# Routing ranks: from one pass on VectorE before the routed attention to comparisons on GpSimd and sums on TensorE inside it

## The reference, cut to what matters

```python
def route(x, routing_token, num_tokens, k_eff):
    s = jnp.einsum('bnd,rd->brn', x, routing_token)[:, 0]
    scores = coor_descent(s, k_eff)
    sel_scores, sel_idx = jax.lax.top_k(scores, num_tokens)
    sel_scores = sel_scores + jax.lax.stop_gradient(1.0 - sel_scores)
    return (sel_scores, sel_idx)
...
sq, iq = route(x, rt_q, NQ, min(NQ * FETCH_K, SEQ))          # NQ = 128
...
routed_out = routed_out * sq[..., None]
out = jnp.broadcast_to(null_q, x.shape)
out = out.at[batch_idx, iq].set(routed_out)
return light + out
```

## Time and profile before

| | us |
|---|---|
| median of 3 runs (range) | 1854.55 (1852.1 to 1854.71) |
| profiled execution, its own time | 1848.03 |
| its span, first to last instruction | 1845.9 |
| main attention, until its last work | 364.84 |
| from there to the first work of the routed attention | 23.9 |
| routed attention | 388.7 to 749.4 |

### The profile page before, as it was taken

The page is one execution under the profiler, slowest core; times in us unless marked ns, Lnnn a source line. Parts: engine busy times, 40 slices in busy tenths (PEclk is TensorE's granted clock), DMA queues, the critical chain, the costliest instruction groups (busy, mean ns, idle before and its releaser), DMA issues. The chain is left out here.

```text
span 1845.9 us, 32031 instructions
## 1 busy us (share of the span) xinstructions
PE 1560.9 (85%) x10886; PEld 1093.7 (59%) x10886; DVE 1187.4 (64%) x3102; ACT 1005.5 (54%) x2685; POOL 371.4 (20%) x381
## 2 busy tenths in 40 slices
PE   3799999849999999499999986489979946899974
PEld 2477777626666666367777764355546722555543
DVE  5599997547777777544454534666642366889954
ACT  2488887606656666244444443124444435888935
POOL 0100000000000000021111034254403410788820
PEclk9899999959999999699999998689999968899978
DMA  4000000040000000110000012200001120333300
GB/s 136 1 1 1 1 1 1 1 135 1 1 1 1 1 1 1 65 56 10 8 9 10 20 55 87 109 16 13 15 23 46 46 82 7 87 87 86 91 13 23
DMA packets 43837, 62.50 MB, mean 34 GB/s; under 512 B 7432, under 2 KB 29776, under 8 KB 42864
## 3 DMA queue, kind: packets, MB, share of 16 engines
q1 hardware_dynamic: 39136, 51.08, 9.3%
q0 software_dynamic: 4544, 9.38, 1.4%
HBM read 49.88 MB, written 15.75 MB: 36 GB/s over the span
## 5 line engine op out<-in xcount | busy, mean ns | idle before, releaser
L561 ACT ACTIVATE probs<-psum_all,pair_negmax 128x256 f32<-128x256 f32 x512 | 235.4, 472 | 161.6 <-DVE pair_negmax L660 89.6
L1992 POOL TENSOR_TENSOR weighted<-state,c_all 128x512 f32<-128x512 f32 x128 | 163.5, 1297 | 87.4 <-DVE state L2002 72.8
L660 DVE TENSOR_REDUCE pair_negmax<-psum_all 128x2 f32<-128x512 f32 x192 | 123.7, 686 | 67.6 <-PE psum_all L476 67.6
L2002 DVE TENSOR_TENSOR_SCAN state<-decay,psum_all 128x512 f32<-128x512 f32 x128 | 149.0, 1200 | 14.9 <-PE psum_all L1920 12.0
L686 DVE TENSOR_SCALAR probs<-probs,pair_recip 128x256 f32<-128x256 f32 x512 | 146.2, 350 | 4.5
L476 PE MATMUL psum_all<-keys,queryT 64*128 64x256 f32 x1024 | 144.7, 402 | 2.5 <-ACT probs L561 2.5
L572 ACT ACTIVATE probsT<-psum_all 128x512 f32<-128x512 f32 x256 | 139.9, 611 | 0.7 <-PE psum_all L487 0.5
L501 PE MATMUL psum_all<-probsT,values 128*64 128x256 f32 x1024 | 138.8, 392 | 0.0
L487 PE MATMUL psum_all<-ident,probs 128*128 128x128 f32 x1024 | 133.1, 273 | 2.8 <-ACT probsT L572 1.8
L487 PEld LDWEIGHTS psum_all<-ident,probs 128*128 128x128 f32 x1024 | 119.1, 141 | 18.1 <-issue 4.4
L476 PEld LDWEIGHTS psum_all<-keys,queryT 64*128 64x128 f32 x1024 | 92.9, 190 | 54.5 <-issue 46.4
(11 more groups left out here) (361 smaller groups left out, 3201.2 us busy)
## 6 DMA issues: line engine op xcount, KB each, us to landing
c_all<-c_rows SPq DMA_DIRECT2D x64, 256.0 KB, 3.3
slots<-slot_fill_dram SPq DMA_DIRECT2D x2, 2535.0 KB, 14.2
ring<-slots SPq DMA_DIRECT2D x18, 260.0 KB, 2.8
keys<-found SPq DMA_DIRECT2D x16, 256.0 KB, 4.6
up<-up_dram SPq DMA_DIRECT2D x1, 2048.0 KB, 7.7
down<-down_dram SPq DMA_DIRECT2D x1, 2048.0 KB, 12.5
up<-up_dram SPq DMA_DIRECT2D x1, 1408.0 KB, 6.0
found<-values,dest POOLq DMA_INDIRECT x78, 2.2
```

Source lines behind the costliest of these rows:

```text
L561: nc.scalar.activation(k.probs[:, 2 * (u % PAIR_BUF) + j, t, :], k.psum[score_bank(u, j)][:, SEQ * t:SEQ * (t + 1)], ACT.Exp, bias=k.pair_ ...
L660: nc.vector.reduce_max(k.pair_negmax[:, u % 2, SUB * j:SUB * (j + 1)], src, AXX, negate=True).then_inc(s.negmax_ready, 1)
L1992: nc.gpsimd.tensor_tensor(w.weighted[:, u % RING, :], w.state[:, u % RING, :], w.c_all[:, u // L3_DC % C_RING, :], ALU.mult)\
L2002: nc.vector.tensor_tensor_scan(w.state[:, u % RING, :], w.decay[:, u % L3_RING, :, :].rearrange("p b n -> p (b n)"), k.psum[u % PARTS_RING ...
```

## The change

`route_stage` no longer makes ranks: it ends after the turned scores and weights are saved and row 2 of `route_w` is copied. The broadcast of the scores moves to the head of SP's list in the routed attention, ahead of the two table fills, into a buffer of its own. There GpSimd does `compare(q)` for each sequence: for both halves t of tokens, with token 128t + partition as "theirs", it marks which tokens have a lower score, which have the same, and multiplies the latter by a mask of later tokens, six operations on 128x256 values with a semaphore wait between the second and third. A new job "rank" at step 8q+2 sums the marks over partitions on TensorE: 8 matmuls with a block of marks as weights and a 128x2 tile of ones as moving data, accumulated over 4 matmuls into two columns for each half. VectorE reads the sums and writes rows 1 and 0 of `route_w` (two operations on 128x2 values). `compare(q)` for q of 1 and more waits until the rank job of q-1 is made, and stands between `copy_inputs(q+1)` and `copy_inputs(q+2)` in GpSimd's list. Four semaphores are new in `pair_attention_stage` (used twice), and one goes from `route_stage`.

```diff
@@ -348,6 +348,7 @@
         for i, job in enumerate(values):
             (before if q == 0 else late[PAIRS * q - 5 + i]).append(job)
         if ffn:
+            late[PAIRS * q + 2].append(("rank", q, 0))
             late[PAIRS * (q + 1) + 1].append(("null_probs", q, 0))
     return before, early, late
 
@@ -377,7 +378,7 @@
 
     def last_input_job(q):
 
-        return [job for job in order if job[1] == q and job[0] != "null_probs"][-1]
+        return [job for job in order if job[1] == q and job[0] not in ("null_probs", "rank")][-1]
 
     def masked(u):
         return ffn and u % PAIRS < PAIRS // 2
@@ -397,7 +398,7 @@
 
         return (1, 0) if u % 3 == 1 else (0, 1)
 
-    with signals(nc, "filled", "x_copied", "job_made", "act_saved_job", "dve_saved_job", "scores_ready", "negmax_ready", "key_max_ready", "probs_ready", "null_args",
+    with signals(nc, "filled", "spread", "ones_set", "tied", "compared", "x_copied", "job_made", "act_saved_job", "dve_saved_job", "scores_ready", "negmax_ready", "key_max_ready", "probs_ready", "null_args",
                  "null_exps", "sums_ready", "recip_ready", "null_weights", "probs_normed", "turned", "turned_saved", "values_weighed", "out_saved",
                  "output_made", "output_added", "route_dve", "route_act", "act_step", "dve_step") as s:
 
@@ -418,14 +419,33 @@
                     for i, src in enumerate((c.w.xlT, c.w.xrT) if ffn else (k.xnT,)):
                         nc.gpsimd.tensor_copy(k.xb[:, q % 2, i, :], src[:, cols]).then_inc(s.x_copied, 1)
 
+                def compare(q):
+                    if q == 0:
+                        pool.wait_ge(s.spread, 16)
+                    else:
+                        wait_made(pool, ("rank", q - 1, 0))
+                    for t in range(SUB):
+                        theirs = k.route_cols[:, 0, t, q:q + 1]
+                        nc.gpsimd.tensor_scalar(c.w.compare[:, t, :], c.w.scores_all[:, q, :], theirs, None, ALU.is_lt).then_inc(s.compared, 1)
+                        nc.gpsimd.tensor_scalar(c.w.compare[:, SUB + t, :], c.w.scores_all[:, q, :], theirs, None, ALU.is_equal).then_inc(s.tied, 1)
+                        pool.wait_ge(s.tied, SUB * q + t + 1)
+                        nc.gpsimd.tensor_tensor(c.w.compare[:, SUB + t, :], c.w.compare[:, SUB + t, :], c.w.later[:, t, :], ALU.mult)                            .then_inc(s.compared, 1)
+
+                if ffn:
+                    nc.gpsimd.memset(c.w.ones[:, :], 1.0).then_inc(s.ones_set, 1)
                 copy_inputs(0)
                 copy_inputs(1)
                 for q in range(SEQS):
+                    if ffn:
+                        compare(q)
                     if q + 2 < SEQS:
                         copy_inputs(q + 2)
 
             @block.sync
             def _(sp):
+                if ffn:
+                    sp.dma_start(c.w.scores_all[:, :, :].rearrange("p b n -> p (b n)"),
+                                 k.scratch.rearrange("b n -> (b n)").partition_broadcast(P)).then_inc(s.spread, 16)
                 for slots in fills:
                     sp.dma_start(slots, k.dram["slot_fill"]).then_inc(s.filled, 16)
                 if fills:
@@ -455,6 +475,13 @@
                     elif what == "null_scores":
                         for t in range(SUB):
                             last = nc.tensor.matmul(jb[:, PAIRS * t:PAIRS * (t + 1)], xb[:, 1, P * t:P * (t + 1)], c.w.null_w[:, :], start=True, stop=True)
+                    elif what == "rank":
+                        pe.wait_ge(s.ones_set, 1)
+                        pe.wait_ge(s.compared, 2 * SUB * (q + 1))
+                        for t in range(SUB):
+                            for n in range(2 * SUB):
+                                last = nc.tensor.matmul(jb[:, 2 * t:2 * t + 2], c.w.compare[:, n, P * t:P * (t + 1)], c.w.ones[:, :],
+                                                        start=(n == 0), stop=(n == 2 * SUB - 1))
                     elif what == "null_probs":
                         pe.wait_ge(s.null_weights, PAIRS // 2 * (q + 1))
                         for t in range(SUB):
@@ -610,6 +637,7 @@
                         nc.vector.tensor_tensor(rows, rows, yb[:, 0:SEQ].rearrange("p (t n) -> p t n", t=SUB), ALU.add).then_inc(s.output_added, 1)
                         return
 
+                    wait_saved(dve, ("rank", q, 0))
                     for t in range(SUB):
                         i = SUB * q + t
                         step.add(nc.vector.scalar_tensor_tensor(k.mix[:, t, :], yb[:, SEQ + P * t:SEQ + P * (t + 1)], k.route_w[:, 0, i:i + 1],
@@ -640,6 +668,10 @@
                         ins = nc.vector.tensor_copy(k.values[:, q % 2, i // 2, 0:CHUNK], jb[:, :])
                     elif what == "values":
                         ins = nc.vector.tensor_copy(k.values[:, q % 2, :, 0:HD], jb[:, 0:SUB * HD].rearrange("p (t n) -> p t n", t=SUB))
+                    elif what == "rank":
+                        ranks, tiles = jb[:, 0:2 * SUB:2], slice(SUB * q, SUB * (q + 1))
+                        nc.vector.tensor_scalar(k.route_w[:, 1, tiles], ranks, float(NQ), None, ALU.is_ge)
+                        ins = nc.vector.scalar_tensor_tensor(k.route_w[:, 0, tiles], ranks, float(NQ), k.route_cols[:, 1, :, q], ALU.is_lt, ALU.mult)
                     else:
                         ins = nc.vector.tensor_copy(k.null_scores[:, q % 2, :, :].rearrange("p t h -> p (t h)"), jb[:, 0:SUB * PAIRS])
                     ins.then_inc(s.dve_saved_job, 1)
@@ -722,7 +754,7 @@
 def route_stage(nc, k, w):
 
 
-    with signals(nc, "dve_step", "scored", "exped", "weighted", "sent", "spread", "turned", "cols_saved") as s:
+    with signals(nc, "dve_step", "scored", "exped", "weighted", "sent", "turned", "cols_saved") as s:
         with nc.Block() as block:
             @block.vector
             def _(dve):
@@ -739,30 +771,8 @@
 
                 nc.vector.tensor_copy(k.route_cols[:, :, :, :].rearrange("p a t r -> p (a t r)"), k.psum[0][:, 0:4 * 16]).then_inc(s.cols_saved, 1)
                 dve.wait_ge(s.cols_saved, 1)
-                dve.wait_ge(s.spread, 16)
-                n = 0
-                for b in range(BATCH):
-                    for t in range(SUB):
-                        mine = k.route_cols[:, 0, t, b:b + 1]
-                        i = SUB * b + t
-                        if n >= 2:
-                            dve.wait_ge(s.dve_step, step.n - 2)
-                        step.add(nc.vector.tensor_scalar(w.compare[:, n % 2, :], w.scores_all[:, b, :], mine, 0.0, ALU.is_gt, ALU.add,
-                                                         accum_out=k.rank[:, 0, i:i + 1]))
-                        step.add(nc.vector.scalar_tensor_tensor(w.compare[:, 2 + n % 2, :], w.scores_all[:, b, :], mine, w.earlier[:, t, :],
-                                                                ALU.is_equal, ALU.mult, accum_out=k.rank[:, 1, i:i + 1]))
-                        n += 1
-                step.wait()
-                step.add(nc.vector.tensor_tensor(k.rank[:, 0, :], k.rank[:, 0, :], k.rank[:, 1, :], ALU.add))
-                step.wait()
-                selected = k.route_w[:, 0, :]
-                step.add(nc.vector.tensor_scalar(selected, k.rank[:, 0, :], float(NQ), None, ALU.is_lt))
-                step.add(nc.vector.tensor_scalar(k.route_w[:, 1, :], k.rank[:, 0, :], float(NQ), None, ALU.is_ge))
-                step.wait()
                 by_token = k.route_cols[:, 1, :, :].rearrange("p t r -> p r t")
-                step.add(nc.vector.tensor_tensor(selected.rearrange("p (b t) -> p b t", t=SUB), selected.rearrange("p (b t) -> p b t", t=SUB),
-                                                 by_token[:, 0:BATCH, :], ALU.mult))
-                step.add(nc.vector.tensor_copy(k.route_w[:, 2, :].rearrange("p (b t) -> p b t", t=SUB), by_token[:, BATCH:2 * BATCH, :]))
+                nc.vector.tensor_copy(k.route_w[:, 2, :].rearrange("p (b t) -> p b t", t=SUB), by_token[:, BATCH:2 * BATCH, :])
 
             @block.scalar
             def _(act):
@@ -775,8 +785,6 @@
                 sp.wait_ge(s.scored, 1)
                 sp.dma_start(k.scratch, k.logits[0:BATCH, :]).then_inc(s.sent, 16)
                 sp.wait_ge(s.sent, 16)
-                sp.dma_start(w.scores_all[:, :, :].rearrange("p b n -> p (b n)"),
-                             k.scratch.rearrange("b n -> (b n)").partition_broadcast(P)).then_inc(s.spread, 16)
 
             @block.tensor
             def _(pe):
...
-            null_out=sb("null_out", [P, P]), earlier=k.gate_cmp[:, 0:4, :, :].rearrange("p j t e -> p (j t e)").rearrange("p (t n) -> p t n", t=SUB), compare=k.masked_scores[:, :, :, :].rearrange("p i t n -> p (i t) n"),
-            scores_all=k.probs[:, 0:4, :, :].rearrange("p i t n -> p (i t) n"))
+            null_out=sb("null_out", [P, P]), later=k.gate_cmp[:, 0:4, :, :].rearrange("p j t e -> p (j t e)").rearrange("p (t n) -> p t n", t=SUB),
```

(6 more changed lines are left out.)

## The result

| | before | after |
|---|---|---|
| median (range, runs) | 1853.05 (1850.81 to 1855.94, 13) | 1857.98 (1856.18 to 1861.18, 13) |
| profiled execution, its span | 1848.03, 1845.9 | 1856.27, 1854.0 |

The ratio is 1.0027 [1.0019, 1.0036], so 4.9 us slower in the medians; +7.6 was forecast.

The account below looks back on a forecast made before the run. The emptied stretch of `route_stage` was taken as fully on the path, the routed attention as bound by TensorE from its second step. -17.6 + 15.0 + 0.55 + 9.6 = +7.6 us on 1854.55 gave 1862.1, range 1851 to 1868.

Parts of the forecast that it names:

- rival B: Routed attention: VectorE keeps the port through its L686 chain, or L686 does not contend; stall 1.8, total 1854.4 us; chance 0.30.
- Removed, -17.6: End of `route_stage`: the wait for the broadcast and VectorE's comparisons go, so it ends 17.6 us earlier.
- Rank jobs, +15.0: TensorE, step 8q+2 of the routed attention: 8 added jobs of 1.87 us each, uncovered, cost 15.0 us.
- C (hidden): TensorE's rank job loads slip under long matmuls, so the 15.0 falls away: 1847.1 us; chance 0.07.
- E (slow accumulation): Rank job matmuls accumulating into two columns wait for each other, 3.2 us a job: 1872.7 us; chance 0.06.
- Semaphores and memset, +0.55: Stage ends and input copies: 7 more semaphores to clear cost 0.5 us, a memset about 0.05.
- Marks against their due time: GpSimd's compare(q), about 3.8 us, is done well before the rank job needs its marks: nothing directly.
- Rival F: Marks reach the rank job late, from a broadcast behind the fills or slow comparisons: 1865 us or more; chance 0.02.
- rival D: Head of the routed attention: TensorE's clock stays up, shrinking it by up to 8.6 us, to 1853.5; chance 0.05.
- Turns at the port, +9.6: Steps 8q+5: VectorE operations wait for GpSimd's comparisons at a shared port; TensorE stalls 1.6 us in 6 sequences, 9.6.
- A: The forecast itself: VectorE and GpSimd take turns at the port; 1862.1 us, own range 1858.5 to 1867; chance 0.50.

Follow-up runs that it names:

- bf16_marks: Changed kernel with marks and ones stored as bf16 instead of fp32; ratio to the kernel before 0.9945 [0.9932, 0.9959].
- marks_once: Changed kernel with GpSimd comparing only for sequence 0, later rank jobs counting those marks again; ratio to the kernel before 1.0004 [0.9990, 1.0017].
- six_tt: Changed kernel with all six GpSimd operations of compare(q) made tensor_tensors, ranks meaningless; ratio to the kernel before 1.0047 [1.0031, 1.0063].
- later_start: Changed kernel with compare(q) waiting for its own sequence's null scores instead of the previous rank job; ratio to the kernel before 1.0003 [0.9991, 1.0016].

## Why the prediction was right, and where it was not

It forecast slower by 7.6 us; it is slower by 4.9, as forecast in sign, in the range, and as a difference nearer to the forecast than to any rival. (The time itself, 1857.98, lies 4.1 under the 1862.1 and 3.6 over rival B's 1854.4, since the median of before came out 1.5 lower than the one reckoned with.) That nearness is in part luck: the port was priced 5.5 us too high, and about 3 us of the measured loss lie in no step that the prediction speaks of. In the stretch itself the loss is 1.8 us, nearer to rival B.

- *Removed, -17.6:* -17.4, of which the difference is the semaphores. Right.
- *Rank jobs, +15.0:* 15.1 in the steps; 1.88 us a job where 1.87 was forecast, out of a load every 0.11 us read from L457 and L1234 (15 x 0.11 + 0.21 is 1.86, so 14.9). Right. `bf16_marks` halves the loads and the matmuls with them and takes 85% off the job, so its time is that of the fp32 loads and their matmuls, which no run separates. Rivals C (hidden) and E (slow accumulation) are out.
- *Semaphores and memset, +0.55:* 0.22 at the end of either attention stage, 4 semaphores each; nothing to be seen of the memset. Right.
- *Marks against their due time:* `compare(0)` started at 374.90 and its marks were used at 399.84. Rival F is out, although a comparison took 0.93 us where I had taken 0.54 from L879: that row is a tensor_scalar too, but it multiplies and adds.
- *Clock, rival D:* the changed kernel has 0.60 in the window 366 to 367 and 0.50 in the next; the clock rises within 393 to 394, 4 us behind the first scores at 389.37, as before within 412 to 413 behind 408.11. Out.
- *Turns at the port, +9.6:* this is the term that was mis-sized. It measured 4.1 in the steps, 3.8 to 3.9 by `marks_once`. The mechanism is there, and for one kind of operation nearly as reckoned (`six_tt`). What failed is that "each L686 waits for one GpSimd operation": only the two products, tensor_tensors, block so. Beside the comparisons an L718 loses 0.22 us at most. Two smaller terms I had at nothing: the interval behind gives back 0.18 each time, and `compare(7)`, which was to meet only maxima and copies out of PSUM, met `add_output`, +0.48. It did because the block is 5.3 us long and not the 3.8 reckoned: in `six_tt`, with 4.4, it ends at 683.49, ahead of L648 at 683.70, and that interval stays at 6.12.

With 3.9 in place of 9.6 the sum is +1.9, and the stretch has +1.8 and +1.9. That is near to rival B's -0.2: its price for the port, 1.8, was 2.1 us too low, mine 5.7 too high. By the line that the prediction drew between A and B, 0.95 us of stall a sequence and 5.7 in all, the 0.87 and the 4.1 measured fall on B's side. In mechanism neither holds: L686 does contend, and it does not wait for one whole operation each time. The rule that I had drawn on (the Trainium skill, "SBUF — State Buffer", section "Who interferes with whom") has any operation of GpSimd block for its whole length; here the tensor_tensor does (0.81 us from one L718's start to the next) and the comparing tensor_scalar does not.

What is left open: in two sets of runs the changed kernel is 5.0 and 4.1 us slower than before, both intervals (from 3.5 and 2.2 us) beginning above the 1.8 and 1.9 that the stretch shows. So part of the measured loss has no place in the steps that I could find. Of the other kernels two show the like (`marks_once` and `later_start`, 2.7 and 2.8 above their stretch), and the rest lie within some 2 us of theirs, on either side. Whether something behind the routed attention really is 2 to 3 us slower, or the sets of runs differ by so much, the profiles can't tell, since those stages take from 1090.1 to 1102.2 us over the profiles, and in none of the later sets of runs were both kernels profiled.

## What to carry to other kernels

Before moving work from a stage that runs alone into one that is bound by an engine, look whether the engine that did it can go on doing it there: VectorE had 11.5 us a sequence to spare, the move alone is worth 17 us, and handing the sums to TensorE, the bound, gave 15 of them back. If TensorE must sum 0/1 marks, store them as bf16: a job fell from 1.88 to 0.29 us. And when two engines contend, list what waits behind the delayed instruction: four normalisations that took 0.96 us longer (and small operations, 0.43 longer) cost 0.69 us a sequence in one step, and four that took 0.97 longer cost nothing three steps later, by one changed wait.

## What the runs showed of the hardware

- On GpSimd a comparing tensor_scalar with a column of scalars takes 0.93 us for 128x256 fp32 values, a tensor_tensor 0.73, a copy 0.40.
- VectorE's tensor_scalar with one SBUF input (0.27 us apart when free) is held up for the whole of a GpSimd tensor_tensor (0.73 apart), but by 0.08 to 0.16 us on the average beside comparing tensor_scalars: by 0.13 to 0.22 if it starts in the first 0.66 us of one, not at all if it starts 0.73 us or more behind its start.
- A bf16 load of 128x128 weights comes every 0.036 us with two moving columns, an fp32 one every 0.117, and fp32 needs two of them for a matmul.
